# Attention with causal softmax: row maxima transposed in fp32, their two parts made after the transposition and sent by two transfers

## What is computed

```python
qkv = x @ qkv_w.T + qkv_b
q, k, v = jnp.split(qkv, 3, axis=-1)                  # then 16 heads of 8 channels each
att = jnp.einsum('bhqd,bhkd->bhqk', q, k) / np.sqrt(HEAD_DIM)
att = jnp.where(causal[None, None], att, -jnp.inf)
att = jax.nn.softmax(att, axis=-1)
out = jnp.einsum('bhqk,bhkd->bhqd', att, v)
```

## Time and profile before

| what | value |
|---|---|
| times of the three runs | 1232.43, 1236.88, 1237.95 us |
| span of the profiled execution, first to last instruction | 1230.5 us |
| own time of the profiled execution | not given beside the span |
| attention in the profile | from the start to about 597 us |
| TensorE, VectorE, ScalarE, POOL busy over the span | 945.4, 841.5, 597.4, 601.8 us |
| granted TensorE clock, mean over the span | 0.926 |

### The profile page before, as it was taken

How to read it: one execution, slowest core, us unless ns; L and a number is a source line. 1 busy time by engine, 2 the same in 40 slices (tenths; PEclk the granted TensorE clock), 3 DMA queues, 4 the chain that set the end, 5 groups by cost and what they waited for, 6 DMA issues and landing times. The chain is left out here.

```text
span 1230.5 us, 26032 instructions
## 1 busy us (share of the span) xinstructions
PE 945.4 (77%) x6984; PEld 719.4 (58%) x6985; DVE 841.5 (68%) x2383; ACT 597.4 (49%) x1283; POOL 601.8 (49%) x813
## 2 busy tenths in 40 slices
PE   3999999999999999999435667777777677777400
PEld 2566666666666666666234556667666666667400
DVE  3788999999999999989799543334333343334388
ACT  1566666666666666666477222222222222222186
POOL 5234443443444344434468455555556555555363
PEclk9999999999999999999879898899989998988855
DMA  3222222222222222222222111111111111111194
GB/s 95 57 62 68 64 56 61 66 60 57 64 66 56 56 68 65 54 58 63 79 102 68 54 42 39 36 38 38 38 36 39 40 38 36 38 38 38 47 253 138
DMA packets 87798, 76.07 MB, mean 62 GB/s; under 512 B 10096, under 2 KB 82544, under 8 KB 87376
## 3 DMA queue, kind: packets, MB, share of 16 engines
q1 hardware_dynamic: 78768, 56.32, 17.3%
q0 software_dynamic: 8704, 17.84, 5.1%
q10 hardware_dynamic: 288, 1.46, 0.3%
HBM read 32.07 MB, written 17.30 MB: 40 GB/s over the span
## 5 line engine op out<-in xcount | busy, mean ns | idle before, releaser
L346 POOL TENSOR_SCALAR_AFFINE_SELECT probs<-probs 128x512 f32<-128x512 f32 x256 | 156.9, 638 | 304.3 <-ACT probs L426 304.3
L568 DVE TENSOR_REDUCE neg_max<-ps_s 128x2 f32<-128x512 f32 (+1 forms) x384 | 257.6, 680 | 40.9 <-PE ps_s L685 23.9
L426 ACT ACTIVATE probs<-ps_st 128x1536 f32<-128x1536 f32 x128 | 185.8, 1452 | 59.7 <-PE ps_st L698 59.7
L1112 POOL DMA_INDIRECT picked_rows<-rows_out,idx x136 | 134.4, 988 | 155.7 <-ACT rows_out L1140 92.4
L1165 DVE COPY h_t<-ps_h 128x384 f32<-128x384 f32 x136 | 75.7, 556 | 161.8 <-PE ps_h L1248 86.5
L1106 POOL DMA_INDIRECT xg<-x_rows,idx x136 | 132.2, 972 | 54.8 <-issue 30.8
L1240 PE MATMUL ps_y<-w_sb,h_t 128*128 (+1 forms) x816 | 127.6, 297 | 39.8 <-DVE h_t L1165 27.5
L1240 PEld LDWEIGHTS ps_y<-w_sb,h_t 128*128 128x128 f32 (+1 forms) x816 | 117.0, 208 | 51.1 <-issue 50.4
L1131 ACT ACTIVATE act_a<-ps_a 128x352 f32<-128x352 f32 x136 | 63.1, 464 | 162.5 <-PE ps_a L1219 99.8
L684 PE MATMUL ps_s<-k_pad,q_dense 128*128 128x512 f32 x256 | 130.8, 511 | 8.3 <-DVE neg_max L568 8.2
L1140 ACT ACTIVATE rows_out<-ps_y 128x128 f32<-128x128 f32 x136 | 37.7, 278 | 166.4 <-PE ps_y L1240 85.2
(11 more groups left out here) (179 smaller groups left out, 2365.2 us busy)
## 6 DMA issues: line engine op xcount, KB each, us to landing
k_pad<-k_dense SPq DMA_DIRECT2D x128, 96.0 KB
q_pad<-q_dense SPq DMA_DIRECT2D x128, 96.0 KB
pick<-picked_rows SPq DMA_DIRECT2D x32, 256.0 KB, 3.6
xt_sb<-xt SPq DMA_DIRECT2D x32, 128.0 KB, 2.1
x_sb<-x SPq DMA_DIRECT2D x32, 128.0 KB, 2.1
x_rows<-y_all SPq DMA_DIRECT2D x8, 512.0 KB, 2.9
out<-normal SPq DMA_DIRECT2D x16, 256.0 KB, 2.4
w_raw<-w SPq DMA_DIRECT2D x2, 1408.0 KB, 7.5
```

Source lines behind the costliest of these rows:

```text
L346: last = pool.affine_select(out=part, in_=part, compare_op=ALU.is_ge, fill=0.0, base=0, pattern=[[0, GROUP], [1, P]], channel_multiplier=-1)
L426: act.activation(probs[:, g % 2, :], ps_st[:].rearrange("p k f -> p (k f)"), ACT.Exp, scale=float(HEAD_DIM) ** -0.5).then_inc(exp_done[g], 1)
L568: nc.vector.tensor_reduce(out=dst, in_=src, axis=AX.X, op=ALU.max, negate=True).then_inc(max_done[h][k], 1)
L1112: pool.indirect_dma_start(out=out_rows, out_offset=bass.IndirectOffsetOnAxis(ap=idx[:, it.ring(-2, IDX), 1:2], axis=0), in_=rows_out[:, it ...
```

## The change

The maxima are laid out by head and block instead of block and head, so that TensorE can transpose the 8 columns of fp32 maxima as they are. The transposition waits for the maxima of piece 2 instead of the two operations behind them. ScalarE's copy of the 8 transposed rows makes the rounded part (`round_shift`, told by `shift_rounded`). VectorE makes the rest from PSUM and that copy (`split_shift`, told by `shift_taken`): a subtraction of 8 partitions and 128 columns, placed after the maximum of piece 1 of the step. SP sends the parts by two transfers of one row each, the first after `shift_rounded`, the second after `shift_taken`; `products` waits for both. VectorE's two operations of 128 partitions and 8 columns are gone.

```diff
-        neg_max = sb("neg_max", [P, 2, BLOCKS, GROUP])
-        shift = sb("shift", [P, 2, 2, GROUP, BLOCKS], F32R)
-        shift_t = sb("shift_t", [2 * BLOCKS * GROUP, 2, P], F32R)
+        neg_max = sb("neg_max", [P, 2, GROUP, BLOCKS])
+        shift_t = sb("shift_t", [BLOCKS * GROUP, 2, 2, P], F32R)
...
         def shift_columns(h):
 
-            return ps_o[0:2 * BLOCKS * GROUP, L + (h % 2) * P:L + (h % 2 + 1) * P]
+            return ps_o[0:BLOCKS * GROUP, L + (h % 2) * P:L + (h % 2 + 1) * P]
...
@@ SP, in each step
                         p = it.ring(off)
-                        it.wait(shift_taken[h], off)
-
                         it.wait(st_done[h], off - 2)
-                        sp.dma_start(
-                            q_pad[SHIFT_ROW:SHIFT_ROW + 2, p, h, :, :].bitcast(F32).rearrange(
-                                "s j (k q) -> s (j k) q", k=BLOCKS),
-                            shift_t[:, h % 2, :].bitcast(F32)).then_inc(shift_landed[h], 16)
+                        for part, ready in enumerate((shift_rounded[h], shift_taken[h])):
+                            it.wait(ready, off)
+                            sp.dma_start(
+                                q_pad[SHIFT_ROW + part:SHIFT_ROW + part + 1, p, h, :, :].bitcast(F32).rearrange(
+                                    "s j (k q) -> s (j k) q", k=BLOCKS),
+                                shift_t[:, h % 2, part, :].bitcast(F32)).then_inc(shift_landed[h], 16)
...
@@ ScalarE, first in each step
-            def take_shift(it, h, off):
+            def round_shift(it, h, off):
                 it.wait(shift_made[h], off)
 
-                it.wait(shift_landed[(h + 2) % GROUPS], off if h >= 2 else off - 1, 16)
-                act.activation(shift_t[:, h % 2, :], shift_columns(h), ACT.Copy).then_inc(shift_taken[h], 1)
+                it.wait(shift_landed[(h + 2) % GROUPS], off if h >= 2 else off - 1, 2 * 16)
+                act.activation(shift_t[:, h % 2, 0, :], shift_columns(h), ACT.Copy).then_inc(shift_rounded[h], 1)
...
@@ VectorE
+            def split_shift(it, h, off):
+                if not it.has(off):
+                    return
+                it.wait(shift_rounded[h], off)
+                nc.vector.tensor_tensor(shift_t[:, h % 2, 1, :], shift_columns(h),
+                                        shift_t[:, h % 2, 0, :].bitcast(F32), ALU.subtract).then_inc(shift_taken[h], 1)
...
+                            if k == 0:
+                                two_before(shift_made, it, h, off)
                             nc.vector.tensor_reduce(out=dst, in_=src, axis=AX.X, op=ALU.max,
                                                     negate=True).then_inc(max_done[h][k], 1)
+                        if k == 1:
+                            split_shift(it, *shift_group(g))
                         choose(it, 3 * g + k)
...
-                    if it.has(off):
-
-                        two_before(shift_made, it, h, off)
-                        it.wait(max_done[h][2], off)
-                        m = neg_max[:, h % 2, :, :].rearrange("p k j -> p j k")
-                        nc.vector.tensor_copy(shift[:, h % 2, 0, :, :], m).then_inc(shift_hi[h], 1)
-                        it.wait(shift_hi[h], off)
-                        nc.vector.tensor_tensor(shift[:, h % 2, 1, :, :], m, shift[:, h % 2, 0, :, :].bitcast(F32),
-                                                ALU.subtract).then_inc(shift_ready[h], 1)
...
@@ TensorE
             def turn_shift(it, g, h, off):
-                it.wait(shift_ready[h], off)
+                it.wait(max_done[h][2], off)
...
-                nc.tensor.transpose(shift_columns(h), shift[:, h % 2, :, :, :].rearrange("p s j k -> p (s j k)").bitcast(F32),
-                                    ident).then_inc(shift_made[h], 1)
+                nc.tensor.transpose(shift_columns(h), neg_max[:, h % 2, :, :].rearrange("p j k -> p (j k)"), ident).then_inc(shift_made[h], 1)
...
-                it.wait(shift_landed[g], 0, 16)
+                it.wait(shift_landed[g], 0, 2 * 16)
```

More of the change, by code:

```diff
@@ L214, in attention @@
         max_done = [[sem(f"max_done{g}{k}") for k in range(3)] for g in range(GROUPS)]
-        shift_hi = [sem(f"shift_hi{g}") for g in range(GROUPS)]
-        shift_ready = [sem(f"shift_ready{g}") for g in range(GROUPS)]
+        shift_rounded = [sem(f"shift_rounded{g}") for g in range(GROUPS)]
         shift_landed = [sem(f"shift_landed{g}") for g in range(GROUPS)]
@@ L420, in visit @@
                     if it.has(off):
-                        take_shift(it, h, off)
+                        round_shift(it, h, off)
                     if it.has(0):
@@ L566, in visit @@
                             src = bank.rearrange("p (h t) -> p h t", t=P if k == 0 else L)
-                            dst = neg_max[:, h % 2, 0, :] if k == 0 else neg_max[:, h % 2, 1, 2 * k - 2:2 * k]
+                            dst = neg_max[:, h % 2, :, 0] if k == 0 else neg_max[:, h % 2, 2 * k - 2:2 * k, 1]
+                            if k == 0:
+                                two_before(shift_made, it, h, off)
                             nc.vector.tensor_reduce(out=dst, in_=src, axis=AX.X, op=ALU.max,
                                                     negate=True).then_inc(max_done[h][k], 1)
+                        if k == 1:
+                            split_shift(it, *shift_group(g))
                         choose(it, 3 * g + k)
```

## The result

The changed kernel takes 1248.78 us in the median of six runs (1243.51 to 1250.19), the kernel before, beside it on the same chip, 1234.66 us (1230.02 to 1238.58). The ratio is 1.0114, 95% interval 1.0083 to 1.0145: slower by 1.1%, 14.1 us. The forecast had 21 us more.

What follows compares the result with a forecast made beforehand. TensorE led before; afterwards SP's queue was to bound the attention: 9.91 + 1.52 = 11.43 us to `products` of g3, plus 6.98, a visit of 18.41. Over 30 visits 21.3 us more, a median of 1258, range 1240 to 1274.

Steps and rivals of the forecast that it cites:

- The sign and the mechanism: Attention: slower, because SP's queue from `k_pad` to `products` of g3 sets the pace; a visit 0.71 us longer.
- The two transfers of the train: SP queue, g1 and g2: one added shift transfer each, issue 0.66 plus gap 0.10 us, together 1.52 us a visit.
- The landing: From a shift transfer's issue to TensorE's weight load: left at 2.03 us, no gain from the halved size.
- The rest: TensorE's path from `products` of g3 to the next `k_pad`: 7.27 us less the 0.29 shift wait, 6.98.
- The subtraction: VectorE, each step: the new 128-column subtraction with one operand in PSUM takes 0.29 us, ends 0.17 and 0.55.
- That the two losses do not add: g3: `products` late by about 1.0 us for the queue, `weighted` held 0.78 by the subtraction; only the larger counts.
- The second case: Rival: the late subtraction before `weighted` in g3 sets the pace, not the queue; visit 18.16 us, 1251 in all; chance 0.20.
- Faster: Rival: VectorE's load was the true bound, so lightening it gains 0.42 us a visit, giving 1224; chance 0.10.
- `k_pad`'s landing as the next limit: Scores of g2 need `k_pad`'s landing, 5.08 us after its start, so TensorE can use only 0.13 of 0.48 us.
- The cover of g3's transfers: The second transfer of g3 lands 4.5 us after the turn, against a 4.4 us step; late `products` covers the rest.

Runs made afterwards that it cites:

- high part only: The changed kernel without the low part: no subtraction, one transfer a step, `weighted` waiting for ScalarE's copy; 17.12 us a visit, ratio 0.9841 to before.
- kernel before with two transfers: The kernel before, old shift kept, its one shift transfer of two rows cut into two of one row; 18.01 us a visit, ratio 1.0082.
- early subtraction: The changed kernel with the new subtraction after the maximum of piece 0 instead of piece 1; 18.12 us a visit, ratio 1.0120 to before.
- high part sent alone: The changed kernel without the low part's transfer, subtraction still made after piece 1 and awaited by `weighted`; 17.98 us a visit, ratio 1.0074 to before.
- high part alone, early subtraction: The changed kernel without the low part's transfer and with the subtraction after piece 0; 17.15 us a visit, ratio 0.9849 to before.
- both together: The changed kernel with both shift transfers sent together after the subtraction, which stays after piece 1; 18.30 us a visit, ratio 1.0202 to before.

## Why the prediction was right, point by point

**The sign and the mechanism** held. The visit is bounded by the SP queue from `k_pad` to `products` of g3, as forecast, with the wait in g3 of 0.90 us (forecast 0.5 to 1) and VectorE 93.1 us lighter over the whole program (841.5 to 748.4; forecast 100). The time of 1248.78 lies in the range, 9 us under the forecast of 1258. Against the kernel beside it the change cost 14.1 us where the sum had 21.3.

**The terms of the sum**, a visit:

- The two transfers of the train: 1.52 us forecast, 9.42 - 7.88 = 1.54 measured. The issue (0.66 us) and the gap (0.10; 0.11 measured) were taken rightly; that source and destination were the same tiles was the better ground than the short issue of `x_sb`.
- The landing: 2.03 us from issue to the weight load forecast, 1.84 measured. This is the term that was mis-sized most, 0.19 us, and part of that is a misread row. The weight load at 593.89 in the earlier trace rows names the transfer, but `products` also waits for ScalarE's exponential, which the matmul beside it names and which ended at 593.77, 0.12 us before the load. In the last visit of the kernel with the high part only, the exponential ends at 576.39 and the load follows after the same 0.12 us, 2.01 us after the issue of a transfer of one row. First two rows: before; last three: high part only.

```profile
592.32 1.45 ACT L426 ACTIVATE probs<-ps_st 128x1536 f32<-128x1536 f32 x1 [0.49 <-PE ps_st L698]
593.92 0.70 PE L697 MATMUL ps_st<-q_pad,k_dense 128*128 128x512 f32 x2 [0.41 <-ACT probs L426]
```

```profile
574.50 0.64 SPq L289 DMA_DIRECT2D q_pad<-shift_t  x1
574.94 1.45 ACT L422 ACTIVATE probs<-ps_st 128x1536 f32<-128x1536 f32 x1 [0.52 <-PE ps_st L686]
576.51 0.30 PEld L685 LDWEIGHTS ps_st<-q_pad,k_dense 128*128 128x128 f32 x2 [0.65 <-DMA q_pad<-shift_t]
```

  So 2.03 us was an upper bound. What is left is the transfer's own gain, which I had put at nothing. The semaphore events kept in the traces, which no row prints, put the last one 1.92 us after the start of the issue for the transfer of two rows (before: the median of 128, nine of ten within 1.89 to 1.95) and 1.81 for one row (high part only: nine of ten within 1.77 to 1.83): 0.11 us sooner. The number of events differs too: a transfer leaves 3 before (96 for 32 transfers of a step), an early one and 2 more, and 9 after (576 for 64), an early one and 8 more. Whether what stands behind these 3 and 9 events or the halved size makes the 0.11 us no run tells apart.
- The rest: 7.27 - 0.29 = 6.98 forecast, 6.90 measured. The size held, its reason did not: I had put the 0.29 down to the lighter VectorE, and the kernel before with two transfers, with VectorE as heavy as ever, has 6.88. TensorE's wait in g3 is enough to take it away.
- Together 18.41 forecast, 18.13 measured. Over 30 visits the difference of 0.28 is 8.4 us, more than the miss of 7.2; the extra loss in the first visits, which the sum did not have, goes the other way.

**The subtraction** took 0.27 us (forecast 0.29); the mean of 92 is 269 ns. All 92 took 268 to 270 ns, so neither of the forecast's ends, 0.17 and 0.55, was met. The timeline of POOL and of VectorE in g1 of the visit shown has one operation whose time stays beside POOL's and one whose time does not:

```profile
423.18 1.19 POOL L351 TENSOR_SCALAR yc<-y,mv 128x128 f32<-128x128 f32 x2 [0.17 <-DVE mv L511]
424.58 0.40 POOL L354 COPY y_all<-yc 128x256 f32 x1 [0.22 <-POOL yc L351]
```

```profile
424.22 0.27 DVE L561 TENSOR_TENSOR shift_t<-ps_o,shift_t 8x128 fp32r<-8x128 f32 x1
424.42 0.15 DVE L551 TENSOR_TENSOR hit_b<-cst,chosen_b 128x16 f32<-128x16 f32 x1
424.61 0.40 DVE L554 SCALAR_TENSOR_TENSOR rest_b<-hit_b,chosen_b 128x16 f32<-128x16 f32 x1
```

The subtraction starts inside POOL's work and stays at 0.27 us, as do all 23 of the 92 that have POOL's L351 beside them. L554 takes 0.40 us here, where its median is 0.18: from 134 to 533 us it is 0.40 in every second visit (12), in which POOL's copy (L354) starts 0.03 us before it, and 0.18 in the 11 between, in which the copy starts 0.07 to 0.09 us after it. The old subtraction (L581) is alike in the trace of before: 122 of its 128 took 0.53 us or more, each with POOL at work beside it for at least 0.51 us (118 of them with L346), and the other six 0.166 to 0.168, four of them with no POOL operation beside them. No new subtraction of the 92 stands beside the operation of the old L346, and no kernel was run with POOL's work taken away, so that POOL makes the old 0.55 us is read from this coincidence alone, and why the new one keeps its 0.27 was not shown.

**That the two losses do not add** was the step most worth testing, and it held: the subtraction was 0.15 us behind the queue (0.22 in the forecast), and removing one of the two gave 0.01 or 0.15 us. The second case, put at 0.20 with 18.16 us a visit, names the time almost exactly, by luck, and the cause wrongly: the early subtraction changed nothing. Its own figure, tried in the high part sent alone, was 17.98.

**Faster** was put at 0.10 on the ground that VectorE's load was the bound. It was not, but the price of that case (0.42 us a visit, 1224) was near what the kernel gives when both limits are lifted (high part alone, early subtraction): 0.56 us, of which 0.14 are beyond the 0.13 + 0.29 that I had allowed, and not traced further.

**`k_pad`'s landing as the next limit** appeared where it was expected, at 427.41 - 422.36 = 5.05 us after the start of its train (5.08 forecast), with a wait of 0.39 us.

**The cover of g3's transfers** held as well, but had less to spare than the text gave it: sending the first half early was part of it, as the run with both together showed (0.29 us of waiting a visit in g0).

## What to carry to other kernels

Before moving work off a busy engine, follow the queue that the new form loads: ten transfers in a fixed order were 0.5 us from the critical path, and one more in each step cost what the saving on VectorE did not return. Cost a queue by the issues in a row (here 0.66 to 0.84 us each) and not by bytes, and put ahead what is needed first. Where two waits of nearly one length end at the same place, removing either can show next to nothing (here 0.01 or 0.15 us a visit, against 0.98 for both); try both together before calling one harmless.

## What the runs showed of the hardware

- Halving a transfer from 8 to 4 KB did not shorten its issue: 0.66 us for two rows of `q_pad`, 0.67 for one. Four issues of 96 KB each (`k_pad`) take 3.34 us, while the one of 128 KB of `x_sb` takes 0.39. The length of an issue did not follow the bytes; what it does follow these runs don't separate, since `x_sb` differs from the others in its source as well as in its form.
- An issue on ScalarE's queue took 0.63 us (median of 128), about as long as on SP, and the engine computed nothing in that time: no ScalarE instruction runs during any of the 128.
- A wait between two issues cost about 0.06 us in the train, where it was already satisfied (0.11 against 0.05 us), which makes 0.12 us a visit; the run that took the wait away, with the early subtraction, gained 0.08 to 0.11.
- A wait in one step went with the end of a wait in another: in the kernel before with two transfers TensorE waited 0.79 us in g3, and its wait of 0.29 us for the shift in g0 vanished although VectorE had as much to do as before. That VectorE catches up meanwhile is the reading that fits.
